# Attention with three turns of six, five and five key tiles per chunk, and two tiles of each chunk summed on VectorE

## What is computed

```python
x = _layernorm(x + _L0_attn_ref(x, ...))    # a gated state space layer
x = _layernorm(x + _L0_ffn_ref(x, ...))     # a linear layer with quantised inputs
x = _layernorm(x + _L1_attn_ref(x, ...))    # the attention
x = _layernorm(x + _L1_ffn_ref(x, ...))     # a mixture of experts

def _L1_attn_ref(latents, ln_gamma, ln_beta, Wq, Wk, Wv, Wo):
    x = ...                                   # layer norm of latents
    q, k, v = ...                             # x @ Wq, x @ Wk, x @ Wv, split into 16 heads
    scores = einsum('bhqd,bhkd->bhqk', q * scale, k * scale)
    weights = softmax(scores, axis=-1)
    out = einsum('bhqk,bhkd->bhqd', weights, v)
    return out.transpose(0, 2, 1, 3).reshape(b, s, HEADS * DIM_HEAD) @ Wo
```

## Time and profile before

| | |
|---|---|
| median of 3 runs | 3421.25 us (3419.8 to 3422.25) |
| the profiled execution | 3422.55 us |
| its span (first to last instruction) | 3420.8 us |
| `attention_pairs`, first to last copy of a chunk's outputs | 739.9 to 3137.4 us, 64 copies |
| PE busy | 3228.0 us, 94% of the span |
| POOL busy | 2707.2 us, 79% |
| DVE busy | 2327.9 us, 68% |
| ACT busy | 1999.1 us, 58% |

### The profile page before, as it was taken

The page is one execution under the profiler, slowest core; times in us unless marked ns, Lnnn a source line. Parts: engine busy times, 40 slices in busy tenths (PEclk is TensorE's granted clock), DMA queues, the critical chain, the costliest instruction groups (busy, mean ns, idle before and its releaser), DMA issues. The chain is left out here.

```text
span 3420.8 us, 57281 instructions
## 1 busy us (share of the span) xinstructions
PE 3228.0 (94%) x20859; PEld 1947.6 (57%) x20861; DVE 2327.9 (68%) x3746; ACT 1999.1 (58%) x3828; POOL 2707.2 (79%) x1342
## 2 busy tenths in 40 slices
PE   6995899399999999999999999999999999998998
PEld 2554455155555555555555555555555555554898
DVE  3887688666667666666666776666676666664664
ACT  6984797245555555555655665555555555554454
POOL 1881386079999999999999999999999999996333
PEclk9997899699999999999999999999999999999999
DMA  2220121210000000000000000000000000000000
GB/s 51 91 87 21 53 89 59 59 28 1 4 1 4 4 1 4 1 4 1 4 1 4 7 7 7 1 4 1 4 1 4 4 1 2 1 1 22 20 24 12
DMA packets 66053, 59.95 MB, mean 18 GB/s; under 512 B 7786, under 2 KB 49332, under 8 KB 65716
## 3 DMA queue, kind: packets, MB, share of 16 engines
q1 hardware_dynamic: 63970, 55.93, 5.6%
q10 hardware_dynamic: 1810, 0.37, 0.1%
HBM read 49.46 MB, written 6.82 MB: 16 GB/s over the span
## 5 line engine op out<-in xcount | busy, mean ns | idle before, releaser
L1610 POOL TENSOR_TENSOR den_g<-den_g,p 128x1024 f32<-128x1024 f32 x888 | 2116.7, 2384 | 142.7 <-ACT p L1532 24.9
L1685 DVE TENSOR_REDUCE quarters<-psum 128x1 f32<-128x512 f32 x2004 | 1291.4, 686 | 648.8 <-PE psum L1061 604.4
L1532 ACT ACTIVATE p<-psum 128x512 f32<-128x512 f32 x2048 | 1084.4, 600 | 384.8 <-PE psum L1409 337.1
L1422 PE MATMUL psum<-p,v 128*64 128x512 f32 x4096 | 922.8, 592 | 0.0
L1422 PEld LDWEIGHTS psum<-p,v 128*64 128x64 f32 x4096 | 293.3, 137 | 582.0 <-issue 506.9
L1061 PE MATMUL psum<-k_main,q_main 64*128 64x512 f32 x2048 | 449.4, 424 | 6.9 <-DVE quarters L1068 5.6
L652 POOL TENSOR_TENSOR fed_s<-dx,work 128x1024 f32<-128x1024 f32 x128 | 302.2, 2363 | 179.2 <-POOLq L593 160.6
L1409 PE MATMUL psum<-row_shift,row_ones 64*128 64x512 f32 x2048 | 415.8, 389 | 0.0
L1409 PE MATMUL psum<-q_main,k_main 64*128 64x512 f32 x2048 | 413.4, 391 | 2.2 <-PEq L1201 2.2
L1409 PE MATMUL psum<-q_main,k_rest 64*128 64x512 f32 x2048 | 415.1, 390 | 0.0
L1409 PE MATMUL psum<-q_rest,k_main 64*128 64x512 f32 x2048 | 414.7, 390 | 0.0
(11 more groups left out here) (284 smaller groups left out, 3233.3 us busy)
## 6 DMA issues: line engine op xcount, KB each, us to landing
work<-bc_rows SPq DMA_DIRECT2D x128, 256.0 KB, 3.1
resid<-in_resid SPq DMA_DIRECT2D x8, 256.0 KB, 4.2
x_mid<-resid SPq DMA_DIRECT2D x8, 256.0 KB, 2.6
residual<-x_mid SPq DMA_DIRECT2D x8, 256.0 KB, 4.7
x<-x_mid SPq DMA_DIRECT2D x8, 256.0 KB, 2.8
out<-mixed SPq DMA_DIRECT2D x8, 256.0 KB, 2.3
xa<-x_mid SPq DMA_DIRECT2D x4, 256.0 KB, 3.6
w_qkv<-in_Wq SPq DMA_DIRECT2D x16, 64.0 KB, 1.9
```

The costliest lines, as they stand in the source:

```text
L1422: last = nc.tensor.matmul(o_bank[hi(h), :], vv[:, kt, hi(h)], p[:, u % LIVE, h, :], start=(kt == 0), stop=(kt == KT - 1))
L1532: nc.scalar.activation(p[:, u % LIVE, h, :], bank_of["score", u, h], ACT.Exp, scale=float(DH) ** -0.5).then_inc(p_ready, 1)
L1610: nc.gpsimd.tensor_tensor(sums, first, src, ALU.add).then_inc(added_g, 1)
L1685: nc.vector.reduce_max(quarters[:, to % 2, h, n:n + 1], bank_of["max", u, h], X_AXIS).then_inc(max_read, 1)
```

## The change

- A chunk is done in three turns of 6, 5 and 5 units (`TURN_LENGTHS`) in place of four of 4. A turn of 5 has a max pair ahead of steps 0, 5, 10, 15 and 20, a turn of 6 ahead of steps 0, 5, 9, 14, 19 and 24.
- The uses move: 0 and "values" to the first turn, ahead of and behind the values; "den" and "shift" to the second; "out" ahead of the third turn's values and 1 between its third and fourth unit. DVE makes the shift in the second turn, ahead of `invert`.
- `LIVE` is 12. The tiles 8 and 9 of a chunk are added by DVE in one `reduce_sum` over both buffers (`add_pair`), in the third turn behind `add_outputs`, and POOL adds that sum at the end of the chunk: 14 sums of 128x1024 in place of 15.
- `residual` lies in the first half of `xaT`, and is loaded in the attention's eighth pair in place of at its start. `maxes` has one more wait, on `rounded`, ahead of a chunk's first max pair.

```diff
-LIVE = 10
+LIVE = 12
-TURN = 4
-TURNS = KT // TURN
+TURN_LENGTHS = (6, 5, 5)
+TURNS = len(TURN_LENGTHS)
-USES_AT = {(0, "before"): 0, (0, "behind"): "values", (1, "before"): "den", (2, "before"): "out",
-           (2, "behind"): "shift", (3, "before"): 1}
+END = KT
+USES_AT = {(0, 0): (0, "vector"), (0, END): ("values", "scalar"), (1, 0): ("den", "vector"), (1, END): ("shift", "scalar"),
+           (2, 0): ("out", "vector"), (2, 3): (1, "vector")}
+SUMMED = (8, 9)
+PAIR_AT = 3
-MAX_AT = (0, 5, 11, 16)
+MAX_AT = {5: (0, 5, 10, 15, 20), 6: (0, 5, 9, 14, 19, 24)}
...
-    adds = KT - 1
+    adds = KT - 2
+    added_with = lambda kt: adds if kt in SUMMED else max(kt, 1) if kt < SUMMED[0] else kt - 2
...
+        pair_sum = den_v
+        residual = xaT[:, 0].rearrange("p (c t d) -> p c t d", t=TPC, d=D)
...
+                    if n == 0 and to >= CHUNKS:
+                        pe.wait_ge(rounded, 2 * CHUNKS * (to // CHUNKS - 1) + CHUNKS + to % CHUNKS + 1)
...
                 for i in turns:
-                    first = i * TURN
-                    ahead = range(first + LEAD_S, min(first + LEAD_S + TURN, len(units)))
+                    first = first_of(i)
+                    ahead = range(first + LEAD_S, min(first_of(i + 1) + LEAD_S, len(units)))
                     steps = (step for u in ahead for step in score_steps(u))
-                    for n in range(MAX_AT[-1] + 1):
-                        if n in MAX_AT:
-                            maxes(first + MAX_AT.index(n))
+                    max_at = MAX_AT[TURN_LENGTHS[i % TURNS]]
+                    for n in range(max_at[-1] + 1):
+                        if n in max_at:
+                            maxes(first + max_at.index(n))
                         next(steps, None)
-                    if (i, "before") in at_turn:
-                        use(at_turn[i, "before"])
-                    for u in range(first, first + TURN):
-                        values(u)
-                    if (i, "behind") in at_turn:
-                        use(at_turn[i, "behind"])
+                    for place in places(i):
+                        if (i, place) in at_turn:
+                            use(at_turn[i, place])
+                        if place != END:
+                            values(first + place)
...
                 for u, (g, kt) in enumerate(units):
-                    if kt == 0 or (g == GC - 1 and kt >= BY_VECTOR):
+                    if kt == 0 or kt in SUMMED or by_vector(g, kt):
                         continue
...
+                    if kt == KT - 1:
+                        pool.wait_ge(pair_done, g + 1)
+                        pool.wait_ge(added_g, n)
+                        nc.gpsimd.tensor_tensor(sums, sums, flat(pair_sum[:]), ALU.add).then_inc(added_g, 1)
+                        n += 1
...
+                def add_pair(g):
+                    at = g * KT + SUMMED[0]
+                    dve.wait_ge(p_ready, 2 * (at + 2))
+                    if g:
+                        dve.wait_ge(added_g, (g - 1) * adds + added_with(SUMMED[1]))
+                    two_tiles = p[:, at % LIVE:at % LIVE + 2].rearrange("p k h q -> p (h q) k")
+                    nc.vector.reduce_sum(flat(pair_sum[:]), two_tiles, X_AXIS).then_inc(pair_done, 1)
```

More of the change, by code:

```diff
@@ L1257, in hand_out_banks @@
     for i in turns:
-        first = i * TURN
-        steps = (step for u in range(first + LEAD_S, min(first + LEAD_S + TURN, count)) for step in score_steps(u))
-        for n in range(MAX_AT[-1] + 1):
-            if n in MAX_AT:
-                maxes(first + MAX_AT.index(n))
+        first = first_of(i)
+        steps = (step for u in range(first + LEAD_S, min(first_of(i + 1) + LEAD_S, count)) for step in score_steps(u))
+        max_at = MAX_AT[TURN_LENGTHS[i % TURNS]]
+        for n in range(max_at[-1] + 1):
+            if n in max_at:
+                maxes(first + max_at.index(n))
             next(steps, None)
-        use(i, "before")
-        now += TURN * SUPPOSED["values"]
-        use(i, "behind")
+        for place in places(i):
+            use(i, place)
+            if place != END:
+                now += SUPPOSED["values"]
     return bank_of, in_front
@@ L1355, in _ @@
                         sp.wait_ge(use_full, use_of[1, CHUNKS * pair - 1] + 1)
+                    if pair == PAIRS - 1:
+                        for c in range(CHUNKS):
+                            sp.dma_start(residual[:, c], tokens(x_in, 0, c)).then_inc(residual_loaded, 16)
                     for i, w in enumerate(("Wq", "Wk", "Wv")):
@@ L1426, in use @@
                 def use(k):
[L1427 removed]
+                    what, g, *_ = uses[k]
                     bank = bank_of["use", k]
@@ L1565, in _ @@
                         normalise_tokens(job_at[i // TURNS - 1])
+                    for k in uses_of(i):
+                        if uses[k][3] != END:
+                            read_use(k)
                 copy_outputs(GC - 1)
                 act.wait_ge(o_copied, GC)
-                act.wait_ge(freed_by_scalar, sum(place == "behind" for *_, place in uses))
+                act.wait_ge(freed_by_scalar, sum(reader == "scalar" for *_, reader in uses))
             @block.gpsimd
@@ L1686, in _ @@
                                                      X_AXIS).then_inc(max_read, 1)
-                    k = at_turn.get((i, "before"))
-                    if k is not None and uses[k][0] == "out":
-                        add_outputs(k)
-                    elif k is not None and uses[k][0] == "den":
-                        invert(k)
-                        normalise(k)
-                    elif k is not None:
-                        take_rest(k)
-                    if i % TURNS == SHIFT_MADE_AT // TURN and g + 1 < GC:
+                    if first_of(i) < g * KT + SHIFT_MADE_AT <= first_of(i + 1) and g + 1 < GC:
                         dve.wait_ge(max_read, 2 * (g * KT + SHIFT_MADE_AT))
@@ L1699, in _ @@
                         make_shift(nc, st, quarters[:, (g + 1) % 2], maxima[:], shift).then_inc(shift_ready, 1)
+                    pair_due = i % TURNS == TURNS - 1 and not by_vector(g, SUMMED[0])
+                    for k in [*uses_of(i), None]:
+                        if pair_due and (k is None or uses[k][3] >= PAIR_AT):
+                            add_pair(g)
+                            pair_due = False
+                        if k is None:
+                            continue
+                        what, reader = uses[k][0], uses[k][4]
+                        if reader != "vector":
+                            continue
+                        if what == "out":
+                            add_outputs(k)
+                        elif what == "den":
+                            invert(k)
+                            normalise(k)
+                        else:
+                            take_rest(k)
                     if i % TURNS == 0 and g in job_at:
@@ L1707, in _ @@
                                 st.link(nc.vector.tensor_tensor(flat(den_v[:]), first, flat(p[:, u % LIVE]), ALU.add))
-                dve.wait_ge(freed_by_vector, sum(place == "before" for *_, place in uses))
+                dve.wait_ge(freed_by_vector, sum(reader == "vector" for *_, reader in uses))
         nc.all_engine_barrier(sems_to_clear=sem_range(su.sems))
```

85 lines of the change are left out of this document (48 added, 37 removed).

## The result

| | before | after |
|---|---|---|
| median of 5 runs | 3421.43 us | 3436.09 us (3434.0 to 3440.52) |
| ratio | | 1.0042, 95% interval 1.0029 to 1.0056 |
| the profiled execution, its span | 3422.55, 3420.8 us | 3440.52, 3438.5 us |
| first to last copy of a chunk's outputs (63 distances) | 739.9 to 3137.4 us | 744.4 to 3156.9 us |
| one chunk, mean of these | 38.056 us | 38.294 us |

The changed kernel is slower by 14.7 us, where 3440 us, some 18.6 more than before, was forecast. The 63 chunk distances account for 15.0 us (2412.5 against 2397.5). So chunks are compared, not spans.

The account below looks back on a forecast made before the run. PE was taken to bound the kernel. Span 3420.8 - 19.8 (a turn less) + 38.3 (closer max pairs) = 3439.3 us, adjusted by +1.75 - 1.3 to about 3440 us; forecast 3433 to 3447, 8-in-10 range 3411 to 3456.

Parts of the forecast that it names:

- What bounds the kernel: Attention chunks: PE sets the time, busy 38.26 of 38.26 us in a chunk; POOL comes next at 36.17.
- A turn less gives 0.31 us a chunk: Changes of form around a turn: 0.10 + 0.12 + 0.09 us saved a chunk, 19.8 us over 64 chunks.
- the way out: From a turn's last max pair to the use: 0.35 us in place of 0.23, so 0.12 us a turn.
- The closer max pairs cost 0.61 us a chunk: Max and score pairs wait for banks not yet released: 38.3 us in all, lower bound 11 us.
- All four places: Turn of 6: max pair at 11 waits 0.22 us, score unit from 25 0.13; each turn of 5: unit from 20 0.13.
- ACT's second bank: Behind a score unit's last pair: free at 1.58 us, usable at 1.81; the max pair at 11 has 1.61.
- The sum on DVE, POOL, shift, buffers at nothing: Third turn's 2.3 us sum hidden by 3.0 us of cover; POOL, shift, buffers off the path: no cost.
- the shift's late pair: One late pair a chunk, waiting for ACT's two copies of the shift and a bank: stays, one turn earlier.
- The gain of the form wins: Rival: waiting weight loads still hide behind the matmul in flight; 3412.7 us, or 3401.5 without waits; chance 0.13.
- Only the max pair at 11 waits: Rival: the three 0.13 us waits vanish, 3415.5 us, or 3428 with half of each; chance 0.16.
- DVE becomes late: Rival: DVE's sum takes 4.7 us, delaying use 1's rest and the next first max pair; 3488 us; chance 0.07.
- a tail on DVE: Rival: second turn, 0.1 to 0.3 us a chunk where `make_shift` is long; 3446 to 3459 us; chance 0.12.

Follow-up runs that it names:

- a_pool: Changed kernel with GpSimd making all 15 sums of a chunk again, no sum on DVE: 3437.57 us, ratio 1.0045 to the kernel before.
- b_half: Kernel before with DVE reading 256 of the 512 columns of each max bank: 3408.81 us, ratio 0.9962.
- a_half_even: Changed kernel with DVE reading half of each max bank and the turn of six's max pairs at 0, 5, 10, 15, 20, 24: 3385.29 us, ratio 0.9894.
- a_half: Changed kernel with DVE reading 256 of the 512 columns of each max bank: 3390.10 us, ratio 0.9908 to the kernel before.
- a_tt: Changed kernel with DVE's sum of two tiles as one two-input tensor_tensor in place of reduce_sum: 3434.45 us, ratio 1.0035 to the kernel before.
- b_close: Kernel before with only each turn's third max pair moved closer (MAX_AT 0, 5, 9, 16 in place of 0, 5, 11, 16): 3471.18 us, ratio 1.0144.
- b_merge_10: Kernel before with one copy for the shift rows and the third max pair one pair earlier (MAX_AT 0, 5, 10, 16): 3416.43 us, ratio 0.9985.
- b_merge: Kernel before with the shift rows copied by one activation over partitions 0 to 65 in place of two: 3416.12 us, ratio 0.9981.

## Why the prediction was right

**What bounds the kernel**: right. PE sets the time in every run; taking GpSimd's sum away or giving it back (`a_pool`) moves nothing.

**A turn less gives 0.31 us a chunk**: right as a sum, by parts with some luck. `b_half` against `a_half_even` shows 0.33 us. Of that, pairs and ways in and out together give 0.17 us, not 0.22; the values' last distance gives 0.11, not 0.09; and use 1 gives 0.05, where the forecast had "no term". The first was too large because the way out was priced at 0.12 us: it is 0.10 with half reads (0.324 less 0.227 us), and the ways out that stay grew by 0.01 to 0.02 each. Two errors of 0.05 us cancelled.

**The closer max pairs cost 0.61 us a chunk**: right in place and nearly in size. All four places that the table of banks named wait, and no fifth: 0.20 + 0.13 + 0.12 + 0.12 = 0.57 us. The links of the chain of release can be read one by one in after's trace: 0.44 us from pair 6 to DVE's read, 0.69 us of reading, 0.12 us to the load, and 0.11 us to the matmul, the last inferred from the load that follows. The term was 0.04 too large, 0.02 of it at the max pair at 11. By the terms as measured, 63 x 0.57 - 64 x 0.33 = 14.8 us, and the medians differ by 14.7; by the forecast ones it was 18.5. So the mechanism was right, and both terms were off by a few hundredths of a microsecond in the same direction of the sum. That the first sum comes within 0.1 us of the medians is closer than the runs can tell.

**A step that was wrong without harm**: ACT's second bank was taken to be usable 1.81 us behind the start of the pair that ends a score unit; in `a_half` only 0.07 us were lost where that gives 0.19. The 1.15 us for two exponentials rested on 3.22 us that the earlier trace rows don't show: it is the distance of PE's pairs that end the first and the fourth unit. Measured are 1.09 us, and 0.05 us from ACT's end to the load where DVE's 0.12 was used. In the changed kernel DVE's bank hid this.

**The sum on DVE, POOL, shift, buffers at nothing**: right. The sum takes 2.31 us (2.29 from the row of 2048 elements), the idle times behind it are 0.96 and 0.83 us. `a_pool` and `a_tt` change it and its length without a change of the time. The second turn's tail on DVE would delay the third turn's first read, and with it the max pair at 6, where the shift's late pair stands too. That read starts 0.55 us behind the turn's first max pair in the mean, against 0.54 in the other turns, and over 0.58 us in 6 of 61 turns (0.72 at most); the distance ahead of pair 7 is 0.291 us, about as long as before (0.295). So the tail shows in a tenth of the chunks and costs nothing that can be seen.

**The rivals.** "The gain of the form wins" falls with `b_close`: a waiting load doesn't hide. "Only the max pair at 11 waits" falls with the table of after. "DVE becomes late" falls with the length of the sum, and "a tail on DVE" with the third turn's first reads. Parts of the change that no run takes back alone are the 12 buffers, the places of the uses other than 1, and the `rounded` wait; the places that wait account for the whole loss without them.

## What to carry to other kernels

When work is moved closer together on the engine that sets the time, write down for each buffer how long it stays taken (fill, signal, read, signal, load) and compare it with the distance to the next that needs it, in the new order: here one number in a table cost 49 us, and a whole turn saved gave 21. A wait that falls short by hundredths of a microsecond is named "issue", or after another engine, in the profile, and PE shows as busy through it; distances between starts tell, busy time doesn't. Before an order is packed more tightly, shorten the reader that sets the pace: the same order of three turns lost 15 us with reads of 0.69 us and won 19 with reads of 0.42 (which leave out half of the keys here, so that run prices the idea and isn't a kernel to use).

## What the runs showed of the hardware

- A DVE read of half a PSUM bank takes 420 ns against 686 for the whole. With the shorter reads PE's distances inside a turn are 0.2288 us in place of 0.2301, and the way out 0.324 in place of 0.349. Late banks explain about 0.01 us of the latter (`b_merge_10`). What the rest is isn't settled by these runs.
- Behind a DVE read the weight load that waited for it starts 0.12 us later (before, `b_close`, after), behind an ACT exponential 0.05 us later (`a_half`). A load usually starts 0.23 us ahead of its pair; one that starts up to about 0.12 us late moved the pair little or not (the last max pairs of before), and later ones moved it by the rest: 0.32 us late cost 0.20 (after), 0.19 late cost 0.07 (`a_half`). That leaves 0.10 to 0.11 us between load and matmul.
- The same projection, four matmuls of the 128\*64 form, took 0.909 us from start to next start behind a max pair and 0.858 us between values (before and after).
- A DVE addition of two SBUF tiles waited for the GpSimd sum in flight in 61 of 63 cases (`a_tt`); the reduce over the same tiles never did (after).
- One ACT copy over 66 partitions takes 0.58 us (`b_merge`), as long as one over 2 partitions.
